# One step of a hand-written TensorE order is moved: the last product of PSUM bank e goes ahead of the third product of bank b

## What is computed

```python
x_q = einsum('oc,bcn->bno', w_qk, y)
x_k = einsum('oc,bcn->bon', w_qk, x)
x_v = einsum('oc,bcn->bon', w_v, x) + b_v[None, :, None]
energy = einsum('bnc,bcm->bnm', x_q, x_k)            # 1024 x 1024 per item
attention = softmax(energy, axis=-1)
attention = attention / (1e-07 + attention.sum(axis=1, keepdims=True))
x_r = einsum('bcn,bnm->bcm', x_v, attention)
out = x + relu(einsum('oc,bcn->bon', w_t, x - x_r) + b_t[None, :, None])
```

## Time and profile before

| | |
|---|---|
| time, median of 3 | 1895.33 us (1894.97 to 1896.39) |
| the profiled execution | 1898.89 us |
| its span, first to last instruction | 1897.1 us |
| mean granted TensorE clock | 0.998 of full speed |
| TensorE matmul busy | 1886.4 us, 99% of the span, 8948 matmuls |
| TensorE weight loads busy | 1565.6 us, 83% |
| VectorE busy | 1503.5 us, 79% |
| ScalarE busy | 1295.6 us, 68% |
| GpSimd busy | 813.2 us, 43% |
| DMA engines, mean busy share | about 15% |

### The profile page before, as it was taken

One profiled execution on the slowest core, in us unless ns is written; L12 is line 12 of the kernel. 1 busy time (PEld: TensorE's weight loads), 2 busy tenths in 40 slices (PEclk: granted clock), 3 DMA queues, 4 the chain that ended last, 5 costly groups with the idle time before them and its releaser, 6 DMA issues.

```text
span 1897.1 us, 26317 instructions
## 1 busy us (share of the span) xinstructions
PE 1886.4 (99%) x8948; PEld 1565.6 (83%) x8948; DVE 1503.5 (79%) x1843; ACT 1295.6 (68%) x1793; POOL 813.2 (43%) x420
## 2 busy tenths in 40 slices
PE   8999999999999999999999999999999999999999
PEld 7888888888888888888888888888888888888887
DVE  5787787887777877778778788777887777877777
ACT  5677666776666776667766677666677666776664
POOL 5443444534445344444344453444534444434430
PEclk9999999999999999999999999999999999999999
DMA  3011111111110111101111111111011110111100
GB/s 105 33 58 45 67 66 44 44 46 65 67 64 25 67 44 67 66 29 60 44 66 67 44 44 45 66 67 62 27 66 45 67 66 28 61 44 66 67 12 34
DMA packets 33946, 101.93 MB, mean 54 GB/s; under 512 B 4208, under 2 KB 4976, under 8 KB 33904
## 3 DMA queue, kind: packets, MB, share of 16 engines
q1 hardware_dynamic: 33360, 101.46, 15.0%
q10 hardware_dynamic: 544, 0.00, 0.0%
HBM read 67.90 MB, written 33.55 MB: 53 GB/s over the span
## 4 chain that ended last, share of the span: by engine, by line
PE 98%; ACT 1%; DVE 1%; POOL 0%; DMA 0%; issue 0%; SPq 0%; DVEq 0%
PE pv L681 36%; PE row_b L589 19%; PE row_a L589 14%; PE pv L657 9%; PE row_b L649 5%; PE row_a L649 5%; PE row_b L640 5%; PE row_a L640 5%; DMA y_raw<-y 0%; PE row_a L688 0%; PE pv L763 0%; PE pv L649 0%; ACT p_sb L300 0%; PE pv L767 0%; ACT y_hi L261 0%
## 5 line engine op out<-in xcount | busy, mean ns | idle before, releaser
L198 POOL TENSOR_TENSOR y_lo<-y_raw,y_hi 128x896 fp32r<-128x896 f32 x128 | 313.5, 2449 | 929.0 <-ACT y_hi L261 929.0
L452 DVE SCALAR_TENSOR_TENSOR p_lo<-p_sb,row_inv,p_hi 128x1024 fp32r<-128x1024 f32 x256 | 325.2, 1282 | 38.2 <-ACT p_hi L308 38.2
L291 ACT ACTIVATE ev<-row_b 128x512 f32<-128x512 f32 x384 | 229.2, 597 | 180.8 <-PE row_b L589 180.7
L445 DVE SCALAR_TENSOR_TENSOR colsum<-p_sb,row_inv,colsum 128x1024 f32<-128x1024 f32 x224 | 333.4, 1488 | 8.6 <-DVE row_inv L435 0.8
L300 ACT ACTIVATE p_sb<-p_sb,neg_max 128x1024 f32<-128x1024 f32 x256 | 294.4, 1153 | 63.6 <-DVE neg_max L427 59.8
L308 ACT ACTIVATE p_hi<-p_sb,row_inv 128x1024 fp32r<-128x1024 f32 x256 | 292.9, 1144 | 18.8 <-PE pv L681 18.8
L681 PE MATMUL pv<-p_hi,z_hi 128*128 128x512 f32 x1024 | 274.7, 390 | 0.0
L681 PE MATMUL pv<-p_lo,z_hi 128*128 128x512 f32 x1024 | 274.0, 389 | 0.3 <-DVE p_lo L452 0.3
L681 PE MATMUL pv<-p_hi,z_lo 128*128 128x512 f32 x1024 | 274.0, 389 | 0.0
L427 DVE CUSTOM_DVE_ANT_0 p_sb<-row_a,ev 128x1024 f32<-128x1024 f32 x128 | 156.6, 1223 | 119.0 <-PE row_a L589 119.0
L681 PEld LDWEIGHTS pv<-p_hi,z_hi 128*128 128x128 f32 x1024 | 192.3, 188 | 41.2
(11 more groups left out here) (129 smaller groups left out, 3582.9 us busy)
## 6 DMA issues: line engine op xcount, KB each, us to landing
x_sb<-x SPq DMA_DIRECT2D x64, 512.0 KB, 3.8
out<-res SPq DMA_DIRECT2D x62, 512.0 KB, 2.9
y_raw<-y SPq DMA_DIRECT2D x64, 256.0 KB, 3.7
y_raw<-y SPq DMA_DIRECT2D x32, 512.0 KB, 3.7
out<-res SPq DMA_DIRECT2D x4, 256.0 KB, 2.0
res<-w_qk SPq DMA_DIRECT2D x1, 256.0 KB, 3.5
res<-w_t_T SPq DMA_DIRECT2D x1, 256.0 KB, 7.2
res<-w_v SPq DMA_DIRECT2D x1, 256.0 KB, 7.5
```

Source lines behind the costliest of these rows:

```text
L198: nc.gpsimd.tensor_tensor(y_lo[:, :, cols], y_raw[:, 1:8, cols], y_hi[:, :, cols].bitcast(FP32), ALU.subtract).then_inc(y_lo_done, 1)
L291: nc.scalar.activation(ev[:, to, :], bank_b, ACT.Copy, scale=scale).then_inc(b_copied, 1)
L445: nc.vector.scalar_tensor_tensor(out=colsum[:, :], in0=p_sb[r][:, :], scalar=inv, in1=colsum[:, :], op0=ALU.mult, op1=ALU.add).then_inc(ac ...
L452: nc.vector.scalar_tensor_tensor(out=p_lo[r][:, :], in0=p_sb[r][:, :], scalar=row_inv[:, j:j + 1], in1=p_hi[r][:, :].bitcast(FP32), op0=AL ...
```

## The change

In `next_pair`, used in slots t = 1, 2 and 3 of every batch item, the call of p3 (last product of bank e, and with it the signal that `row_a` is complete) is moved from behind p7 (third product of bank b) to in front of it. The matmuls, their number and every wait stay. Only the place of three matmuls and of one signal changes, 96 times in the program's run. The first slot (`first_pair`, `very_first_pair`) keeps its order.

```diff
@@ -720,8 +720,8 @@
                 p2(b, t)
                 p6(b, t)
                 pv_pass(b, t - 1, 0, 0, first)
+                p3(b, t).then_inc(row_a_done, 1)
                 p7(b, t)
-                p3(b, t).then_inc(row_a_done, 1)
                 p4(b, t)
                 pv_pass(b, t - 1, 0, 1)
                 pv_pass(b, t - 1, 0, 2)
```

## The result

The changed kernel takes 1917.46 us (median of 5 runs, 1915.52 to 1918.3) beside 1895.4 us for the kernel before (1894.97 to 1897.39). The ratio is 1.0107, 95% interval 1.0097 to 1.0118: 22 us slower, where 8.8 us faster was forecast. The profiled execution of the changed kernel took 1915.52 us with a span of 1913.7 us. It is the fastest of the five, while that of the kernel before (1898.89 us) lies above all of that kernel's other runs, so the two spans are only 16.6 us apart.

The account below looks back on a forecast made before the run. TensorE's matmul starts were taken to bound the kernel; 8.3 us from the slots plus 0.5 from the end of the program gave 8.8 us off 1895.33, so 1886.5 us, range 1885.0 to 1891.0.

Parts of the forecast that it names:

- What bounds the kernel: TensorE, busy 99% of the span: time is the sum of the distances between matmul starts.
- the pace: Undisturbed matmuls start 0.227 us apart; at p7 the first distance is 0.28 us.
- the late load of p7: p7's first weight load, held by ScalarE's copy, is 0.17 us late, of which 0.05 shows.
- the margins of p3 and p7: Spare time of weight loads in the new order: p3 0.33 us (t = 1: 0.98), p7 0.50.
- The 8.3 us of the slots: Gain in t = 1 to 3 from unbroken matmul pace: 64 x 0.09 + 32 x 0.08 us.
- The lower bound (the slow pace stays): Only p7's late start goes, slower matmuls behind it remain: 96 x 0.05 = 4.8 us gained.
- The end of the program: In the last item the earlier row_a reaches the exponentials: 0.5 us gain, bounds 0 and 0.7.
- What it moves behind TensorE: Earlier row_a signal, third copy of b about 0.62 us later, x_lo about 0.25 later; no cost to TensorE while covered.
- the cover: Idle time absorbing lateness: ScalarE 0.68 us behind t = 1, 1.21 behind t = 2; x_lo 0.85; VectorE 1.42.
- Rival 3: Slower: ScalarE's late third copy delays p3's load in t = 2 and 3; 0.21 us each, 1900.4 us, chance 0.04.

Follow-up runs that it names:

- e1: The changed kernel, with GpSimd's y_lo for t = 3 also waiting for this item's last p_lo on VectorE: 1888.33 us, ratio 0.9949 to the kernel before.
- e6: The changed kernel with x_hi ahead of the third copy of b in t = 2 and 3: 1912.46 us, ratio 1.0076 to the kernel before.

## Why the prediction was wrong, point by point

- **What bounds the kernel, the pace, the late load of p7.** Right. All 96 late loads of p7 went, and the margins of p3 and p7 were enough (one load of p3, in the first item, waited 0.07 us).
- **The 8.3 us of the slots.** Right: 0.25 us per item were measured in the changed kernel's slots, which is 8 us, and with the end of the program 9.6 us were gained in e1. The lower bound (the slow pace stays) can be dropped.
- **The end of the program.** 0.5 us taken, 0.7 measured (from the last quadrant sum to the last matmul 10.34 before, 9.65 after).
- **"What it moves behind TensorE", third copy and `x_lo`.** The times are right: `x_lo` starts 0.27 us later against p1 of its slot (0.25 forecast), and the column sum that it holds takes 2.21. The step that failed is the cover. I compared ScalarE's lateness with its idle time before the next slot, and VectorE's with its idle time before the next `energy_out`. Behind t = 3 no next slot follows. VectorE goes on, without idle time, through the second column sum, two `p_lo`, the turn and the next item's `gx_lo`, and what it runs into there is `y_lo` of t = 3 and then the quadrant sum. The forecast put the cost of VectorE's lateness there at nothing; it was 2.14 us against 1.29 of slack, 0.85 us of waiting in each of 31 items. I never laid the rows of GpSimd beside those of VectorE in that stretch. The row `y_lo` 3.18 with a usual 2.14 showed a meeting that had cost GpSimd 1.0 us.
- **Rival 3.** It had the cause (column sum and `x_lo` meet on VectorE and GpSimd) and the wrong law and place. I treated the meeting as a matter of overlap, with the price at the copy of e, and gave it a chance of 0.04. The earlier trace rows could have told the law: `x_lo` runs from 474.41 to 476.84, and the column sum that starts at 475.89 ends at 477.92, 1.08 us behind the end of `x_lo`, in all 62 cases. It waits for the other's end and then does nearly its whole 1.28 us. Under such a law a shift of 0.3 us can cost 1.9 us.
- The quadrant sum's own 0.11 us per item was not thought of. It follows the wait.

The Trainium skill states the law (SBUF — State Buffer, SBUF: two separate sides and Who interferes with whom): the port pair shared by VectorE and GpSimd is an exclusive lock, and between a VectorE instruction with two SBUF inputs and a GpSimd one that reads SBUF whichever starts first has it for the whole instruction, while the other fully blocks. The prediction cited only the shorter sentence of the Trainium skill (GPSIMD Engine Reference, Key points), that the two contend. The runs agree with the full one: `p_lo` 3.15 or 1.28 by the order of the starts, and a reduction with one input untouched.

What the runs leave open: which of two instructions that start within 0.01 us of each other wins by rule. In e6 it was GpSimd in all 31 items, also where its row starts 0.01 us later, and nothing here was tried between 0.01 and 0.03 us.

## What to carry to other kernels

Before a step is moved by some tenths of a microsecond, follow each engine that gets later or earlier to the end of the loop body, not only to its next idle time, and lay VectorE's instructions with two SBUF inputs beside GpSimd's there. Look for instructions that take longer than their usual time, on either engine: they mark a meeting, and its cost can change sides over a margin of 0.1 us. A deliberate order (a wait, or one-input work placed under GpSimd's instruction) is worth more than a margin: it turned +1.1% into -0.5% here.

## What was not expected of the hardware

- The meeting of `y_lo` and the second `p_lo` is decided within 0.05 us. With `y_lo` 0.034 to 0.040 us behind, `p_lo` takes 1.28 and `y_lo` 3.24. With it between 0.014 ahead and 0.012 behind, `p_lo` takes 3.2 and `y_lo` 2.12.
- The held instruction of VectorE ended 1.08 us after the end of GpSimd's, for `colsum` behind `x_lo` and for `p_lo` behind `y_lo` alike.
- A weight load of p7 that is 0.17 us late costs 0.05 us at its matmul and another 0.03 to 0.04 over the matmuls behind it. Both went together in every slot with the new order. The first load of p6 in t = 1 is still 0.12 us late in the changed kernel: its matmul is hardly delayed, but the matmuls behind it too follow in 0.228 to 0.231 instead of 0.227, about 0.02 us in all. That speaks for the late load as the cause of the slow pace.
